# Attention scores from two fp32r parts, two heads at a time on row halves, in place of three bf16 parts with one head at a time

## The chip, the cores and the metric

The kernel runs on one core of one Trainium2 chip. The time is the device time of one launch in microseconds, the median of three runs. "The profiled execution" is one more launch, taken with the hardware profiler; all rows below are from it.

## What is computed

Eight batch elements of 512 rows by 256 columns go through three blocks with residuals: an mLSTM cross attention with four heads (stage A), a mixture of two multi-head attentions of 16 heads of 16 columns each, and a mixture of experts, two of eight chosen by a router (stage C). The change is in the middle block:

```python
n1 = _ln(x, ln1_g, ln1_b)
mha_probs = jax.nn.softmax(jnp.mean(n1, axis=1) @ mha_rw + mha_rb, axis=-1)
q = jnp.einsum('btd,mdhk->mbhtk', n1, mha_wq) + mha_bq[:, None, :, None, :]
kk = jnp.einsum('btd,mdhk->mbhtk', n1, mha_wk) + mha_bk[:, None, :, None, :]
v = jnp.einsum('btd,mdhk->mbhtk', n1, mha_wv) + mha_bv[:, None, :, None, :]
scores = jnp.einsum('mbhtk,mbhsk->mbhts', q, kk) / jnp.sqrt(jnp.float32(KD))
attn = jax.nn.softmax(scores, axis=-1)
ctx = jnp.einsum('mbhts,mbhsk->mbthk', attn, v)
```

Everything is fp32. There are 8 x 2 x 16 = 256 heads of 512 by 512 scores, each with a contraction of only 16.

## The kernel before

Each engine has its own program, written out by hand, and they meet through semaphores. The batch elements are pipelined. A *period* is one batch element's attention; in it run also stage A of the next element and stage C of the one before. A period has 128 slots, one for each score tile: 8 quads of four heads (`qq`), 4 row tiles (`g`), 4 heads (`j`). Three tables (`FIRST`, `MIDDLE`, `LAST`) say at which slot each other piece of work (`p0` to `p7` the K and Q projections, `v0`, `v1` the value projections, `cxT..`, `wo..`, `hid..`, `eo..` of stage C, `kT..`, `cd..`, `num..` of stage A) stands in each engine's program. The digit string `AHEAD` says how many maxima TensorE computes behind each slot. The MIDDLE table serves six of the eight periods.

A head's scores are computed twice. `maximum` (L880) makes a tile of 128 queries by 512 keys, of which VectorE takes the row maxima (L1411). When a quad's 16 tiles are done, `max_rows` transposes the maxima, VectorE splits them in two bf16 rows (L1419, L1421), and SyncE sends these as two more rows of Q (`send_rows`). `score` (L895) then makes the transposed tile of keys by queries with the maximum already subtracted, ScalarE takes the exponential into `prob` (L1710), and `values` (L910) multiplies it by V, four heads at once on column groups of 32, for two row tiles together in every eighth slot.

Fp32 accuracy comes from splitting. ScalarE writes the projection in bf16 (`high`, L1632), VectorE the residue (L1283), GpSimd the second and third bf16 part (`middle_low`, L1861 and L1863). SyncE stacks six products of parts along the contraction (`stack`), 16 rows each, so that one matmul of 96 rows (98 with the maxima) gives the score:

```python
TERMS_K = (0, 0, 1, 1, 0, 2)
TERMS_Q = (0, 1, 0, 1, 2, 0)
```

The first heads of the first element are stacked by matmuls with a choice matrix instead (`pick`, L665 and L680), 48 of them.

PSUM has seven banks for all this and one (`VB`) for the values. `Banks.take` gives each result the bank that is free earliest by the tables, and TensorE waits for its last reader. In the names of the trace all matmul results are `psum`; `kst`, `qst` are the stacks, `mx` the maxima.

## Time and profile before

| | |
|---|---|
| median of three runs | 1407.55 us (1404.99 to 1409.78) |
| profiled execution, whole time | 1407.98 us |
| its span, first to last instruction | 1406.2 us |
| TensorE busy | 1380.4 us, 98% |
| VectorE busy | 1074.6 us, 76% |
| ScalarE busy | 911.4 us, 65% |
| GpSimd busy | 361.0 us, 26% |
| granted TensorE clock, mean | 0.995 |

A busy time is the union of an engine's instructions. TensorE's instructions overlap in its pipeline and their ends are modelled, so the distance from one start to the next says more than the duration. A matmul with fp32 operands leaves two records in the trace, each with a weight load: 1024 matmuls at L910 are 2048 records. A bf16 matmul and a transpose leave one.

### The profile page before, as it was taken

How to read it: one execution, taken by the hardware profiler on the slowest of the kernel's cores; microseconds unless marked ns; L12 is line 12 of the kernel's file. 1: busy time of each engine (PE TensorE's matmuls, PEld its weight loads, DVE VectorE, ACT ScalarE, POOL GpSimd, SP SyncE). 2: the span in 40 equal slices, each digit the busy share in tenths (PEclk: the TensorE clock that was granted, in tenths of full speed). 3: DMA queues.
4: the chain of work that ended last, by engine and by line, in shares of the span. 5: the costliest groups of instructions: out<-in, count | busy, mean ns of one | idle time of the engine just before them, and what ended most of it. 6: DMA issues, size and time to landing. Idle time of an engine off the chain costs nothing. (4 is left out here: it accounts for less than half of the span.)

```text
span 1406.2 us, 22227 instructions
## 1 busy us (share of the span) xinstructions
PE 1380.4 (98%) x7666; PEld 714.5 (51%) x7666; DVE 1074.6 (76%) x2299; ACT 911.4 (65%) x1708; POOL 361.0 (26%) x351
## 2 busy tenths in 40 slices
PE   8999999999999999999999999999999999999989
PEld 6644445554455544456445654555445555354456
DVE  6789878977698777986879777897779868688631
ACT  3367567756667667776577666775676765657751
POOL 7422341302313223113322034132132222221000
PEclk9999999999999999999999999999999999999999
DMA  4065075321744136530662308441174415352002
GB/s 118 17 79 89 2 79 88 67 55 31 105 62 78 59 44 105 86 55 31 85 96 54 69 16 106 76 76 61 28 109 77 75 31 62 46 69 54 21 12 90
DMA packets 92307, 90.15 MB, mean 64 GB/s; under 512 B 16482, under 2 KB 87266, under 8 KB 91294
## 3 DMA queue, kind: packets, MB, share of 16 engines
q1 hardware_dynamic: 92196, 88.73, 38.1%
q8 instruction: 62, 1.02, 0.4%
q14 instruction: 49, 0.40, 0.1%
HBM read 35.05 MB, written 4.25 MB: 28 GB/s over the span
## 5 line engine op out<-in xcount | busy, mean ns | idle before, releaser
L1710 ACT ACTIVATE prob<-psum 128x512 f32<-128x512 f32 x1024 | 560.6, 600 | 317.9 <-PE psum L910 217.2
L1411 DVE TENSOR_REDUCE mx<-psum 128x1 f32<-128x512 f32 x1024 | 640.6, 681 | 77.8 <-PE psum L880 75.3
L895 PE MATMUL psum<-qst,kst 98*128 98x512 bf16 x1024 | 340.7, 382 | 2.3 <-DMA qst<-mrow 1.3
L880 PE MATMUL psum<-kst,qst 96*128 96x512 bf16 x1024 | 305.1, 381 | 5.5 <-DVE resid L1283 2.2
L910 PE MATMUL psum<-prob,vst 128*17 128x512 f32 x2048 | 246.6, 598 | 0.4 <-ACT prob L1710 0.2
L895 PEld LDWEIGHTS psum<-qst,kst 98*128 98x128 bf16 x1024 | 94.9, 98 | 202.8 <-issue 136.5
L880 PEld LDWEIGHTS psum<-kst,qst 96*128 96x128 bf16 x1024 | 97.5, 97 | 127.7 <-ACT prob L1710 17.1
L1861 POOL CAST parts<-resid 128x512 bf16<-128x512 f32 x64 | 39.4, 616 | 404.0 <-DVE resid L1283 404.0
L910 PEld LDWEIGHTS psum<-prob,vst 128*17 128x17 f32 x2048 | 46.7, 96 | 128.8 <-issue 109.8
L867 PE MATMUL psum<-w,cxT 128*128 128x256 f32 x448 | 105.1, 381 | 0.0
L848 PE MATMUL psum<-n2T,x 128*128 128x512 f32 x224 | 102.0, 592 | 0.0
L867 PEld LDWEIGHTS psum<-w,cxT 128*128 128x128 f32 x448 | 85.2, 191 | 15.8 <-DVE mx L1411 1.1
L1863 POOL TENSOR_TENSOR parts<-resid,parts 128x512 bf16<-128x512 f32 x64 | 74.5, 1164 | 5.1
L1757 POOL TENSOR_TENSOR rstd_a<-rstd_a,neghalf 128x4 f32<-128x4 f32 x24 | 24.5, 1031 | 178.8 <-DVE rstd_a L994 100.7
L1831 POOL TENSOR_TENSOR kin<-qbuf,onw 128x1024 f32<-128x1024 f32 (+1 forms) x8 | 16.5, 2059 | 203.4 <-DVE qbuf L1120 201.2
L1419 DVE TENSOR_SCALAR mrow<-psum 16x128 bf16<-16x128 f32 x64 | 17.5, 273 | 63.5 <-PE psum L481 63.5
L848 PEld LDWEIGHTS psum<-n2T,x 128*128 128x128 f32 x224 | 42.3, 190 | 44.9 <-issue 41.8
L730 PE MATMUL psum<-n1T,wk 128*128 128x512 f32 x128 | 60.9, 598 | 0.0
L504 PE MATMUL psum<-wv,n1T 128*128 128x256 f32 x256 | 60.7, 379 | 0.0
L730 PE MATMUL psum<-n1T,wq 128*128 128x512 f32 x128 | 60.2, 592 | 0.0
L504 PEld LDWEIGHTS psum<-wv,n1T 128*128 128x128 f32 x256 | 48.0, 189 | 10.3 <-ACT n2T L1687 1.6
L765 PE MATMUL psum<-wo,cxT 128*128 128x256 f32 x224 | 51.8, 379 | 0.0
(244 smaller groups left out, 1708.3 us busy)
## 6 DMA issues: line engine op xcount, KB each, us to landing
kst<-parts SPq DMA_DIRECT2D x186, 128.0 KB, 4.6
qst<-parts SPq DMA_DIRECT2D x186, 128.0 KB, 5.5
cmat<-G_dram SPq DMA_DIRECT2D x7, 1024.0 KB, 4.7
x<-in_L_ffn_fw SPq DMA_DIRECT2D x14, 512.0 KB, 3.6
w<-in_L_ffn_fw SPq DMA_DIRECT2D x14, 512.0 KB, 4.1
xbuf<-in_x SPq DMA_DIRECT2D x8, 512.0 KB, 5.2
kin<-in_ctx SPq DMA_DIRECT2D x8, 512.0 KB, 4.5
out<-acc SPq DMA_DIRECT2D x7, 512.0 KB, 3.9
```

The lines of the kernel that those rows point to most:

```text
L504: ins = e.matmul(psum[:, u.bank, i * H * KD:(i + 1) * H * KD], n1T[:, kc, t * P:(t + 1) * P], wv[:, kc, m, :], start=kc == 0, stop=kc == K ...
L730: ins = e.matmul(psum[:, u.bank, :], w_[:, kc, m, c * P:(c + 1) * P], n1T[:, kc, :], start=kc == 0, stop=kc == KC - 1)
L765: ins = e.matmul(psum[:, u.bank, 0:E], cxT[:, m, c, t * P:(t + 1) * P], wo[:, m, c, :], start=k == 0, stop=k == M * KC - 1)
L848: ins = e.matmul(psum[:, u.bank, :], w1_of(b, k)[:, kc, f * P:(f + 1) * P], n2T_of(b)[:, kc, :], start=kc == 0, stop=kc == KC - 1)
L867: ins = e.matmul(psum[:, u.bank, 0:E], hidden_of(b, k)[:, f, t * P:(t + 1) * P], w2_of(b, k)[:, f, :], start=f == 0, stop=f == FC - 1)
L880: e.matmul(psum[:, u.bank, :], qst[0:KROWS, h, t * P:(t + 1) * P], kst[0:KROWS, h, :], start=True, stop=True).then_inc(u.full, 1)
L895: e.matmul(psum[:, u.bank, :], kst[0:KROWS + 2, h, g * P:(g + 1) * P], qst[0:KROWS + 2, h, :], start=True, stop=True).then_inc(u.full, 1)
L910: ins = e.matmul(psum[32 * j:32 * j + VW, VB, :], vst[:, g, h, :], prob[:, g % 2, j, :], start=g == 0, stop=g == NT - 1, tile_position=(0, ...
L1411: e.tensor_reduce(mx[:, qq * QUAD + j, t:t + 1], psum[:, u.bank, :], AX, ALU.max).then_inc(u.free, 1)
L1710: e.activation(prob[:, g % 2, j, :], psum[:, u.bank, :], ACT.Exp).then_inc(u.free, 1)
L1861: e.tensor_copy(parts[:, n % 2, 1, :], resid[:, n % 2, :]).then_inc(split_mid, 1)
L1863: e.tensor_tensor(parts[:, n % 2, 2, :], resid[:, n % 2, :], parts[:, n % 2, 1, :], ALU.subtract).then_inc(split_lo, 1)
```

## The change

K and Q are split in two parts instead of three, in fp32r (four bytes): ScalarE writes the first, VectorE the residue straight into the second, and GpSimd's part is gone. Three products of parts (48 rows) replace six (96 rows). Even heads lie in partitions 0 to 63 and odd heads in 64 to 127 of the same free positions, and a matmul of an even head is followed at once by that of the odd head on the other half of the array's rows. For the maxima the two results go to two neighbouring banks (`take_two`), and one VectorE reduction reads both; a quad has 8 such pairs, and `AHEAD` counts pairs. One more VectorE copy a quad (`mxx`) duplicates the maxima before the transpose. Scores are made in pairs at even slots, each in its own bank and with its own exponential. All slot tables are new; `values` stands at slot 0 of eight instead of slot 1. The stack's DMAs are the same in number and bytes with lines twice as long.

```diff
-    TERMS_K = (0, 0, 1, 1, 0, 2)
-    TERMS_Q = (0, 1, 0, 1, 2, 0)
+    TERMS_K = (0, 0, 1)
+    TERMS_Q = (0, 1, 0)
...
-        kst = sb("kst", [P, M * H, S], BF16)
-        qst = sb("qst", [P, M * H, S], BF16)
+        kst = sb("kst", [P, M * H // 2, S])
+        qst = sb("qst", [P, M * H // 2, S])
+        kstR, qstR = kst[:].bitcast(F32R), qst[:].bitcast(F32R)
...
+    def take_two(self, name, until):
...
+        k = min(range(self.count - 1), key=lambda k: (max(self.until(k), self.until(k + 1)),
+                                                      max(self.order[k], self.order[k + 1])))
+        self.counts[k] += 1
+        one = self.uses[name] = self.hold(k, self.counts[k], until)
+        one.both = slice(k, k + 2)
+        return one, self.hold(k + 1, one.n, until, k)
...
             def maximum(b, qq, j, t):
...
-                u = take("max", b, qq, j, t)
-                e.matmul(psum[:, u.bank, :], qst[0:KROWS, h, t * P:(t + 1) * P], kst[0:KROWS, h, :], start=True,
-                         stop=True).then_inc(u.full, 1)
+                u = take_two("max", b, qq, j, t)
+                for par in range(2):
+                    own = slice(HALF * par, HALF * par + KROWS)
+                    ins = e.matmul(psum[:, u.both, :][:, par, :], qstR[own, h // 2, t * P:(t + 1) * P], kstR[own, h // 2, :],
+                                   start=True, stop=True)
+                ins.then_inc(u.full, 1)
...
             def score(b, qq, g, j):
...
-                u = take("score", b, qq, g, j)
-                e.matmul(psum[:, u.bank, :], kst[0:KROWS + 2, h, g * P:(g + 1) * P], qst[0:KROWS + 2, h, :], start=True,
-                         stop=True).then_inc(u.full, 1)
+                us = [take("score", b, qq, g, 2 * j + par) for par in range(2)]
+                for par, u in enumerate(us):
+                    own = slice(HALF * par, HALF * par + KROWS + 2)
+                    e.matmul(psum[:, u.bank, :], kstR[own, h // 2, g * P:(g + 1) * P], qstR[own, h // 2, :],
+                             start=True, stop=True).then_inc(u.full, 1)
...
-                e.scalar_tensor_tensor(out=resid[:, n % 2, :], in0=psum[:, u.bank, :],
+                e.scalar_tensor_tensor(out=partsR[:, n % 2, 1, :], in0=psum[:, u.bank, :],
...
-                e.tensor_reduce(mx[:, qq * QUAD + j, t:t + 1], psum[:, u.bank, :], AX, ALU.max).then_inc(u.free, 1)
+                e.tensor_reduce(mx[:, qq, :, j, t], psum[:, u.both, :], AX, ALU.max).then_inc(u.free, 1)
+                if j == PAIRS - 1 and t == NT - 1:
+                    e.wait_ge(u.free, u.n)
+                    src = mx[:, qq].rearrange("p r h t -> p r (h t)")
+                    e.tensor_copy(mxx[:], src.unsqueeze(2).to_broadcast([P, 2, 2, UNITS])).then_inc(maxima_in, 1)
...
-                e.activation(parts[:, n % 2, 0, :], psum[:, u.bank, :], ACT.Identity,
+                e.activation(partsR[:, n % 2, 0, :], psum[:, u.bank, :], ACT.Identity,
...
-            def middle_low(b, n):
...
-                e.tensor_copy(parts[:, n % 2, 1, :], resid[:, n % 2, :]).then_inc(split_mid, 1)
-                e.wait_ge(split_mid, q_ + 1)
-                e.tensor_tensor(parts[:, n % 2, 2, :], resid[:, n % 2, :], parts[:, n % 2, 1, :], ALU.subtract
-                                ).then_inc(split_lo, 1)
...
-            AHEAD="1300200300314230044012000010100221221000031300001011000104403001"
-                  "0020100321400001210130341010440001130110030202100012010003000000")
...
+            AHEAD="3000100100102220100220201010001000200110000102000002000000120221000"
```

In `pick` there are now 16 matmuls in place of 48.

**TensorE, a stretch of the second period around the experts' first products (`hid`, L848 before and L870 after).** L895 and L920 are scores, L880 and L904 maxima, L910 and L935 values, L481 and L514 transposes, L867 and L889 the experts' second products. Before:

```order
L910 MATMUL psum<-prob,vst 17x512 x8
L895 MATMUL psum<-qst,kst 128x512
L880 MATMUL psum<-kst,qst 128x512 x4
L848 MATMUL psum<-n2T,x 128x512 x2
L895 MATMUL psum<-qst,kst 128x512
L848 MATMUL psum<-n2T,x 128x512 x6
L481 MATMUL psum<-ident,mx 16x128
L895 MATMUL psum<-qst,kst 128x512
L867 MATMUL psum<-w,cxT 128x256 x4
```

Now:

```order
L935 MATMUL psum<-prob,vst 17x512 x8
L920 MATMUL psum<-qst,kst 128x512 x2
L904 MATMUL psum<-kst,qst 128x512 x4
L870 MATMUL psum<-n2T,x 128x512 x2
L904 MATMUL psum<-kst,qst 128x512 x4
L870 MATMUL psum<-n2T,x 128x512 x4
L514 MATMUL psum<-ident,mxx 32x128
L920 MATMUL psum<-qst,kst 128x512 x2
L904 MATMUL psum<-kst,qst 128x512 x2
```

Scores and maxima now stand in twos, one for each half of the rows, between work on the whole array. Each such border is a change of the array's tiling that was none before. Counted over TensorE's whole program, with scores and maxima, L565 and L602 (64 rows), the values and L715 (column groups of 32), L577 (of 64) and all else as four kinds: the kind changed 348 times before and changes 892 times now. Before, 173 changes led into whole-array work (162 of them into a score), 32 into 64 rows, 135 into 32 columns, 8 into 64 columns; now 314, 423, 135 and 20, and 102 of the 314 begin with a transpose. In one middle period it was 44 changes and is 114 now (54 into 64 rows, before 4; 40 into the whole array, before 22), in the first period 40 and 90.

**VectorE, the last maxima of a quad and the row split behind them.** L1411 and L1433 are the maxima. Before:

```order
L1411 TENSOR_REDUCE mx<-psum 128x1 x4
L1431 RECIPROCAL rden<-psum 128x16
L1434 SCALAR_TENSOR_TENSOR cx<-psum,mpc,rden 128x4x64
L1411 TENSOR_REDUCE mx<-psum 128x1 x7
L1419 TENSOR_SCALAR mrow<-psum 16x128
L1421 SCALAR_TENSOR_TENSOR mrow<-psum,mrow 16x128
```

Now:

```order
L1457 RECIPROCAL rden<-psum 128x16
L1460 SCALAR_TENSOR_TENSOR cx<-psum,mpc,rden 128x4x64
L1433 TENSOR_REDUCE mx<-psum 128x2 x4
L1437 COPY mxx<-mx 128x32
L1433 TENSOR_REDUCE mx<-psum 128x2 x2
L1445 CAST mrow<-psum 32x128
L1447 SCALAR_TENSOR_TENSOR mrow<-mrow,low,psum 32x128
```

A reduction now gives two columns, there are half as many, and the copy is new.

## Rows read from the trace of the kernel before

**Rows 1.** The page: span, busy times, busy tenths in 40 slices, granted clock.

```profile
span 1406.2 us, 22227 instructions
...
PE 1380.4 (98%) x7666; PEld 714.5 (51%) x7666; DVE 1074.6 (76%) x2299; ACT 911.4 (65%) x1708; POOL 361.0 (26%) x351
...
PE   8999999999999999999999999999999999999989
...
DVE  6789878977698777986879777897779868688631
...
PEclk9999999999999999999999999999999999999999
```

**Rows 2.** Windows, one a stage: length, then each engine's busy time.

```profile
0.00:81.00 81.00, 72.83 (x384) 48.94 (x385) 55.31 (x140) 29.40 (x63) 42.55 (x62) 0.98 0.22 61
81.00:218.00 137.00, 131.61 (x757) 58.60 (x755) 116.06 (x231) 92.20 (x182) 41.23 (x39) 0.99 0.52 66
...
551.00:716.00 165.00, 164.80 (x935) 84.71 (x933) 132.73 (x284) 113.47 (x212) 42.69 (x39) 1.00 0.42 68
...
1214.00:1347.00 133.00, 131.55 (x706) 61.75 (x707) 92.13 (x185) 88.21 (x159) 17.74 (x15) 0.99 0.26 41
1347.00:1406.00 59.00, 52.48 (x214) 35.60 (x212) 13.92 (x37) 18.29 (x30) 3.35 (x2) 0.97 0.17 54
```

**Rows 3.** Groups by line: busy us, mean ns, idle before and releaser.

```profile
L1411 DVE TENSOR_REDUCE mx<-psum 128x1 f32<-128x512 f32 x1024 | 640.6, 681 | 77.8 <-PE psum L880 75.3
L1710 ACT ACTIVATE prob<-psum 128x512 f32<-128x512 f32 x1024 | 560.6, 600 | 317.9 <-PE psum L910 217.2 <-PE psum L895 98.5
L895 PE MATMUL psum<-qst,kst 98*128 98x512 bf16 x1024 | 340.7, 382 | 2.3 <-DMA qst<-mrow 1.3 <-ACT prob L1710 0.3
L880 PE MATMUL psum<-kst,qst 96*128 96x512 bf16 x1024 | 305.1, 381 | 5.5 <-DVE resid L1283 2.2 <-DVE mx L1411 1.4 <-ACT prob L1710 1.2
L910 PE MATMUL psum<-prob,vst 128*17 128x512 f32 x2048 | 246.6, 598 | 0.4 <-ACT prob L1710 0.2
...
L1863 POOL TENSOR_TENSOR parts<-resid,parts 128x512 bf16<-128x512 f32 x64 | 74.5, 1164 | 5.1
...
L1861 POOL CAST parts<-resid 128x512 bf16<-128x512 f32 x64 | 39.4, 616 | 404.0 <-DVE resid L1283 404.0
...
L665 PE MATMUL psum<-parts,qst 128*96 128x512 bf16 x27 | 6.7, 379 | 0.1
...
L1038 DVE COPY cols<-psum 128x48 f32<-128x48 f32 x8 | 1.5, 193 | 2.1 <-PE psum L550 2.1
```

**Rows 4.** Timeline of TensorE, 501.3 to 504.9 us: start, length, work.

```profile
501.55 0.59 PE L880 MATMUL psum<-kst,qst 96*128 96x512 bf16 x2
501.98 0.38 PE L895 MATMUL psum<-qst,kst 98*128 98x512 bf16 x1
502.20 0.38 PE L880 MATMUL psum<-kst,qst 96*128 96x512 bf16 x1
502.51 1.91 PE L910 MATMUL psum<-prob,vst 128*17 128x512 f32 x16
504.35 0.61 PE L895 MATMUL psum<-qst,kst 98*128 98x512 bf16 x2
504.80 0.38 PE L880 MATMUL psum<-kst,qst 96*128 96x512 bf16 x1
```

**Rows 5.** Timeline of TensorE, 28 to 31 us, a run of row-half pairs.

```profile
28.46 2.06 PE L565 MATMUL psum<-qT,kT 64*128 64x128 f32 x32
```

**Rows 6.** Line L565 by itself, durations min/median/max.

```profile
L565 PEld LDWEIGHTS psum<-qT,kT x256: 182/188/188, 28.5 to 1109.5; 64*128 64x128 f32 x128
L565 PE MATMUL psum<-qT,kT x256: 272/272/373, 28.5 to 1109.6; 64*128 64x128 f32 x128
```

**Rows 7.** Waits: us in total, times, longest.

```profile
POOL parts L1861 <- DVE resid L1283: 404.0, 61, 23.3
ACT prob L1710 <- PE psum L910: 217.2, 115, 5.8
...
DVE mx L1411 <- PE psum L880: 75.3, 85, 2.5
...
PEld psum L880 <- ACT prob L1710: 17.1, 59, 1.7
...
PEld psum L880 <- DVE mx L1411: 6.4, 17, 1.7
```

More of the change, by code:

```diff
@@ L57, in until, with hold @@
         return self.latest[k].until if self.latest[k] is not None else -1000
+    def hold(self, k, n, until, at=None):
+        at = k if at is None else at
+        self.taken += 1
+        self.order[k] = self.taken
+        self.latest[k] = Use(k, n, self.full[at], self.free[at], self.latest[k], until)
+        return self.latest[k]
     def take(self, name, until):
@@ L63, in take @@
         self.counts[k] += 1
-        self.taken += 1
-        self.order[k] = self.taken
-        use = Use(k, self.counts[k], self.full[k], self.free[k], self.latest[k], until)
-        self.uses[name] = self.latest[k] = use
-        return use
+        self.uses[name] = self.hold(k, self.counts[k], until)
+        return self.uses[name]
+    def take_two(self, name, until):
+        assert name not in self.uses
+        k = min(range(self.count - 1), key=lambda k: (max(self.until(k), self.until(k + 1)),
[4 more added lines that the diff above has]
+        return one, self.hold(k + 1, one.n, until, k)
 class Steps:
@@ L378, in build @@
+            SP_S=slots(18, "s4:5 s5:11 s6 s7"),
+            AHEAD="1200102010002002210100120000200210010100000100012000010000021220"
+                  "1120010020010010102100021001001000000100300011000000000010200000")
         for plan in (FIRST, MIDDLE, LAST):
-            assert len(plan["AHEAD"]) == SLOTS and sum(map(int, plan["AHEAD"])) == SLOTS
+            assert len(plan["AHEAD"]) == SLOTS and sum(map(int, plan["AHEAD"])) == SLOTS // 2
             for engine in ("PE", "ACT", "DVE", "POOL", "SP"):
@@ L401, in freed_at @@
             if period is None or not 0 <= period < B:
-                return now + 1
+                return now + (2 if kind == "score" and which[-1] % 2 else 1)
             plan = FIRST if period == 0 else LAST if period == B - 1 else MIDDLE
@@ L478, in take, with take_two @@
                 return u
+            def take_two(*name):
+                both = banks.take_two(name, freed_at(clock[0], *name))
+                for u in both:
+                    if u.was is not None:
+                        e.wait_ge(u.was.free, u.was.n)
+                return both[0]
             def transpose(out_, in_, n):
@@ L1176, in stage_a @@
                     e.wait_ge(u.full, u.n)
-                    e.tensor_copy(qst[0:KROWS, 0, :], psum[0:KROWS, u.bank, :]).then_inc(u.free, 1)
+                    e.tensor_copy(qstR[:, 0, :], psum[:, u.bank, :]).then_inc(u.free, 1)
                 yield "mean"
@@ L1606, in move_pick @@
                 e.wait_ge(u.full, u.n)
-                e.activation((kst, qst)[which][0:KROWS, h, :], psum[0:KROWS, u.bank, :], ACT.Copy).then_inc(u.free, 1)
+                if which:
+                    e.activation(qstR[:, h, :], psum[:, u.bank, :], ACT.Copy).then_inc(u.free, 1)
+                else:
+                    e.wait_ge(shaped, 3)
+                    e.activation(kstR[:, h, :], psum[:, u.bank, :], ACT.Identity, bias=lift[:]).then_inc(u.free, 1)
             def decays(b):
@@ L1814, in stage_a @@
                 e.tensor_copy(mk[:, b % 2, 1, :], sa.rstd[:, 1, :]).then_inc(kept, 1)
-                for n in range(len(PIECES) // M if b else 3):
-                    yield f"s{n}"
-                    middle_low(b, n)
             def weigh(b):
@@ L2119, in sync_program @@
             a.upto(-9)
-            e.wait_ge(ones, 1)
-            for i in range(1, M * H // HC):
-                e.dma_start(kst[KROWS:KROWS + 2, i * HC:(i + 1) * HC, :], kst[KROWS:KROWS + 2, 0:HC, :]).then_inc(ones_in, 16)
+            e.wait_ge(ones, 2)
+            for par in range(2):
+                own = slice(HALF * par + KROWS, HALF * par + KROWS + 2)
+                e.dma_start(kst[own, HP + 1:M * H // 2, :],
+                            kst[own, HP:HP + 1, :].to_broadcast([2, M * H // 2 - HP - 1, S])).then_inc(ones_in, 16)
             until_maxima(a, first)
```

317 lines of the change are left out of this document (156 added, 161 removed), and 12 rows, old and new, of the table DVE_A.

## The prediction

> **What bounds the kernel now.** I read the page first: TensorE is busy in 98% of the span, VectorE in 76%, ScalarE in 65%, and the granted clock is 1.0 nearly throughout, which is the 2.4 GHz level [rows 1]. The windows show where that holds. In a middle period of 165 us TensorE is busy 164.8, VectorE 132.7 (80%), ScalarE 113.5 (69%). In the first period it is less plain, 131.6 and 116.1 of 137 us, VectorE at 85%. The last period is TensorE's again, and the head and the tail (140 us together) hold few scores [rows 2]. The waits say the same: ScalarE waits 217 us for values on TensorE and VectorE 75 us for maxima, while TensorE's waits for a free bank are 17.1 us (ScalarE) and 6.4 us (VectorE) [rows 7]. So TensorE's own stream sets the pace, and what a change takes from it comes off the time, until VectorE is next.
>
> Busy times say nothing of rates on a pipelined engine, so I take distances between starts. Two maxima from 501.55 and the score at 501.98 give 0.215 us for a bf16 matmul of 512 columns. The 16 records of values lie in four groups of four that run at once, 0.43 us a group (from 502.51 to 504.42, less 0.59 for the last one, are 1.32 us for three steps, the first a little longer) [rows 4]. A value matmul is two records [rows 3], so fp32 costs 0.86 us where bf16 costs 0.215, four times as much.
>
> **The change part by part.**
>
> *Scores and maxima.* 2048 matmuls of 0.215 us are 440 us [rows 3, 4]. They become 1024 pairs. That two matmuls on the two row halves run at once is in the trace: L565 issues 32 records, 16 pairs, in 2.06 us. Less the last one's 0.27 and 0.10 for a slow first (below), 15 steps take 1.69 us, 0.113 each [rows 5, 6], where 128 fp32 columns of one matmul alone take 0.107 (256 cycles at 2.4 GHz). A pair thus costs some 0.007 us more than one. What fp32r costs no row shows, and it is the largest unknown. The nearest rows on either side are bf16, 0.215 us for 512 columns, and one fp32 record, 0.43 us [rows 4]. I take 0.215: two records of 0.43 make a full fp32 product of four partial ones, so a partial product costs 0.215, and a split in parts rests on one partial product a matmul. A pair is then 0.222, 1024 are 227 us, and the saving is 213 us. At 0.43 the saving would be nothing (1024 x 0.437 = 447 us, 7 more).
>
> The Trainium skill states in "FP8 and Floating Point Precision", TensorE Precision Notes, that true FP32 takes four passes through the array, and that a reduced-precision mode reads the four bytes and truncates them. The trace agrees with the four passes (0.86 against 0.215 us); no run so far shows the reduced mode. By that page a pair would be at my 0.222.
>
> *Pick.* 48 matmuls of 0.215 become 16: 7 us less, all in the head [rows 3].
>
> *Borders between tilings.* This is what the change adds. From the maximum at 502.20 to the first value is 0.31 us instead of 0.215, and from there to the next score 1.84 instead of 4 x 0.43 = 1.72 [rows 4]. I read 0.095 us for a change in each direction and 0.012 for a first weight load of 17 columns that nothing hides. The count goes from 348 to 892: 544 x 0.095 = 52 us.
>
> *The first weight load behind a border.* With 128 four-byte columns it is longer. L565's matmuls last 272 ns and the first of a run 373 [rows 6]: 0.10 us, and both halves load at once, so a pair pays it once. 391 more entries into the 64-row kind at 0.10 are 40 us. The bound from below is the bf16 score behind a border, 0.012, which would make it 5 us; I take 0.10, since the stacks are now four bytes wide, as in that row. The 314 entries into whole-array work now meet fp32 loads where 162 of 173 met a bf16 score: 212 x 0.10 and 102 transposes at 0.03 (my choice between 0.012 and 0.10) are 24 us, less 2. Elsewhere a load of 188 ns [rows 6] lies beside a pair of 222 and costs nothing; were the pair shorter it would show.
>
> The Trainium skill's "TensorEngine Tiling (Array Packing)", Key Properties, says that changing the tiling mode drains the engine. The trace agrees and gives it the price of 0.095 us. Without that price the sum below would be 52 us lower.
>
> Sum for TensorE: -213 - 7 + 52 + 40 + 22 = -106 us. Of these a middle period has -26.6 (256 x 0.215 less 128 x 0.222), +6.7 (70 borders), +5 and +3, that is -12, from 166 us to 154; the first period -16, the last with the tail -11, the head -7.
>
> *VectorE.* A reduction of 512 elements takes 640.6 / 1024 = 0.626 us. The line's mean of 681 ns against 193 for a copy of 48 columns makes 1.05 ns an element, so 1024 elements take 0.626 + 0.538 = 1.164, and 512 of them 596 us: 45 less. The new copies are 64 x 0.19 = 12 us [rows 3]. VectorE comes to 1042 us, in a middle period to 128.6. The residue writes as much as before.
>
> *GpSimd, ScalarE, SyncE.* GpSimd loses 74.5 + 39.4 = 114 us [rows 3], but it sat waiting 404 us for exactly this work [rows 7]; nothing else becomes earlier than its slot. ScalarE keeps its 1024 exponentials. `stack` waits for two splits in place of three and sends as many bytes. All three at nothing. If a late stack were a cost now, the maxima would wait for it, and the 5.5 us that they wait in all name VectorE and ScalarE [rows 3].
>
> *New waits.* In the first period VectorE, at 112 us after the change, would stand at 93% of the 121 us left. If it keeps its present 85%, the period ends at 132, not 121: 11 us. In the middle VectorE rises from 80 to 83.5% of the period; between the shares that cost 0.2 us (80%) and 5.4 us (85%) of TensorE idle [rows 2] I take 1.5 us, 9 in six. A reduction now holds two banks for 1.2 us, and behind three pairs in one slot (`AHEAD`'s 3) the next score waits for VectorE; these are a few slots a period and I count them in that. Sum: +20.
>
> The profiled execution took 1408 us, 1.8 of it outside its span, and is within 0.5 of the median. 1408 - 106 + 20 = 1322, and I say 1320.
>
> **The rivals.**
>
> *Fp32r streams like an fp32 record (slower).* A pair takes 0.437 us at lines L904 and L920. Speaking for it: every four-byte record in these rows moves at two cycles a column [rows 4, 5], which a limit of reading four bytes would give as well as two partial products would. Against it: then a full fp32 product in two records would need four partial products in the time of two reads, possible only if a read serves two. TensorE's sum is then +7 - 3 + 52 + 40 + 22 = +118 and VectorE is idle more: 1525 us. The change turns from gain to loss when a pair costs 0.222 + 86 / 1024 = 0.306 us. Halves that do not overlap in this format would cost the same.
>
> *VectorE or the banks take over.* If VectorE can't get beyond its 80% of a middle period, a period is 128.6 / 0.8 = 161 us, 5 saved instead of 12; first 5, head 7, last and tail 11: 1408 - 53 = 1355, and to 1395 if pairs of banks are often late. For it: two neighbouring banks of seven are harder to get, and the first period shows TensorE idle at 85%. Against: VectorE's work falls as well. The Trainium skill's tiling page, PSUM Bottleneck, warns of just this: tiling speeds the array and not the emptying of PSUM. Only the first period of this trace bears it out so far.
>
> *Cheap weight loads.* If an fp32r load behind a border costs 0.012 us, 35 us more are saved: 1285, and 1267 without the new waits.
>
> *Nothing changes.* It would take a chain outside TensorE in every period. The page's busy digits are 9 in all but the ends [rows 1]; I give it no case of its own.
>
> **How the numbers follow.** My forecast (1290 to 1345) 0.64, VectorE or banks (1345 to 1395) 0.15, cheap loads (1267 to 1290) 0.08, fp32r at the fp32 rate (about 1525, or some way there) 0.13. The range 1270 to 1375 holds the first, most of the third and somewhat over half of the second, some 0.8. Faster by over 0.3% (about what a measurement of this kernel tells from no change): 0.84, with 0.03 of the last case, where banks cost almost all, going to the same, and 0.13 slower.
>
> **What would show it.** In the new trace: starts of a pair some 7 ns apart and pairs 0.222 us apart; 0.31 from a pair to work of another kind; the first matmul behind a border 0.10 longer; the reduction's busy time at 1.16 us each; middle periods of 154 to 157 us; GpSimd's busy time 114 us lower and no wait for it. Pairs 0.43 apart would make the prediction wrong outright; middle periods near 161 with TensorE waiting for maxima would make it wrong in size.

## The result and the profile after

The changed kernel takes 1509.17 us (median of 4 runs, 1499.85 to 1514.36) against 1408.66 us before (4 runs on the same chip): a ratio of 1.071, 95% interval 1.0651 to 1.0769. It is 7% slower, where the forecast was 1320 us and 6% faster. The profiled execution took 1514.36 us.

The page of the changed kernel, to be laid beside [rows 1]:

```profile
span 1512.3 us, 22468 instructions
...
PE 1400.0 (93%) x7634; PEld 716.7 (47%) x7634; DVE 1071.6 (71%) x1856; ACT 889.6 (59%) x1686; POOL 250.0 (17%) x231
...
PE   9888889999899998999989998999989999899889
...
PEclk9898899899899998999999998989989999899999
```

TensorE is no longer the engine that is always busy: 93% of the span, not 98%. The row of granted clock has gaps in it that were not there. And no other engine has come near its limit; VectorE is at 71%, lower than the 76% before. That is the picture of a kernel that waits in turns, not of one with a new bound.

The groups by line (busy us, mean ns, idle before and its releaser), beside [rows 3]:

```profile
L1744 ACT ACTIVATE prob<-psum 128x512 f32<-128x512 f32 x1024 | 554.0, 602 | 367.2 <-PE psum L935 273.0
L1433 DVE TENSOR_REDUCE mx<-psum 128x2 f32<-128x1024 f32 x512 | 608.1, 1219 | 182.9 <-PE psum L904 180.4
L920 PE MATMUL psum<-qst,kst 50*128 50x512 f32 x1024 | 244.9, 492 | 43.5 <-DMA qst<-mrow 25.5
L935 PE MATMUL psum<-prob,vst 128*17 128x512 f32 x2048 | 282.9, 674 | 0.9 <-ACT prob L1744 0.9
L904 PE MATMUL psum<-kst,qst 48*128 48x512 f32 x1024 | 223.0, 455 | 47.4 <-DVE mx L1433 22.9
```

The reduction is as forecast: 608.1 / 512 = 1.19 us each, where 1.164 was said. What is new stands at the right. TensorE sat idle 43.5 us before scores (2.3 before the change) and 47.4 before maxima (5.5). The values have not changed, yet their mean rose from 598 to 674 ns. That is the clock: those that start at the full clock have a mean of 597 ns in the new trace too.

Windows, one a stage (head, first, the second of the six middle ones, last, tail), beside [rows 2]:

```profile
0.00:79.00 79.00, 68.50 (x352) 47.51 (x353) 53.10 (x138) 25.32 (x55) 36.91 (x65) 0.94 0.23 64
79.00:233.00 154.00, 135.80 (x759) 60.43 (x757) 114.78 (x175) 92.02 (x182) 23.59 (x19) 0.89 0.40 58
...
417.00:597.00 180.00, 168.62 (x944) 85.68 (x943) 133.50 (x230) 112.08 (x213) 29.18 (x23) 0.95 0.36 64
...
1316.00:1454.00 138.00, 127.91 (x718) 61.26 (x718) 90.49 (x138) 86.86 (x162) 10.57 (x7) 0.99 0.23 40
1454.00:1512.00 58.00, 51.96 (x214) 35.23 (x210) 13.90 (x37) 18.12 (x30) 3.32 (x2) 0.97 0.16 55
```

The head is 2 us shorter and the tail 1. The first stage went from 137 to 154 us (132 was forecast; its clock is 0.89), the six middle ones from 165-167 to 176-184, the last from 133 to 138. VectorE's work in a middle stage is what it was (133.5 us beside 132.7), in a stage 15 us longer; the forecast had it fall to 128.6.

TensorE's timeline from 276 to 284 us shows the change at work, and its price:

```profile
276.83 0.51 PE L920 MATMUL psum<-qst,kst 50*128 50x512 f32 x2
...
277.17 0.40 PE L904 MATMUL psum<-kst,qst 48*128 48x512 f32 x2
...
277.41 0.40 PE L920 MATMUL psum<-qst,kst 50*128 50x512 f32 x2
...
278.60 0.50 PE L920 MATMUL psum<-qst,kst 50*128 50x512 f32 x2
...
278.98 0.72 PE L904 MATMUL psum<-kst,qst 48*128 48x512 f32 x4
...
281.61 0.80 PE L920 MATMUL psum<-qst,kst 50*128 50x512 f32 x2 [1.91 <-DMA qst<-mrow]
...
282.34 1.91 PE L935 MATMUL psum<-prob,vst 128*17 128x512 f32 x8
```

Two matmuls of 512 columns, 0.40 us together, start 0.24 us apart from the next two (277.17 to 277.41). So fp32r does run at the bf16 rate, and two halves at once. The first pair behind a border takes 0.34 (276.83 to 277.17), 0.10 more, as forecast. Then the score at 281.61 waits 1.91 us for its maxima rows; and the values behind it move at half speed. Eight of the sixteen records take 1.91 us, where all sixteen took 1.91 in [rows 4].

What the engines waited for (us in total, times, longest), beside [rows 7]:

```profile
DVE mx L1433 <- PE psum L904: 180.4, 163, 5.8
...
PE psum L920 <- DMA qst<-mrow: 25.5, 13, 2.8
...
PE psum L904 <- DVE mx L1433: 22.9, 43, 1.4
...
PEld psum L904 <- ACT prob L1744: 20.6, 33, 1.8
```

VectorE waits for TensorE's maxima for 180 us in all (75 before), and TensorE waits for VectorE's banks: both sit idle, at different moments.

The mean clock of the profiled execution is 0.944. With two levels, 1.2 and 2.4 GHz, the share at the lower one is 2 x (1 - 0.944) = 11%, or 169 us of 1512; before, at 0.994 to 0.996, it was 11 to 17 us. Most of the 29 falls come in or just behind a wait of TensorE, like the one at 281.61 us. Those at 38.5, 332.1 and 1052.3 us come behind rows of short matmuls (L625, L635) that had kept it busy. The four runs of this one kernel show how time and clock go together: 1499.85 us at 0.958, 1507.21 at 0.949, 1511.13 at 0.947, 1514.36 at 0.944, that is about 1.0 us for each 0.001. If that holds up to 1, some 50 us of the 100 lost go with the clock (an estimate from four runs, in which waits and clock may have changed together).

A last view of my own: the distances between successive starts on TensorE, where nothing holds them up, summed for the whole kernel, and what is above them. Before: 1363 us of clean steps, 6 for the lower clock, 40 of longer steps. After: 1279, 68 and 186 (the three overshoot the span by 3 and 21 us). By this view the stream did become 84 us shorter, and some 190 to 210 us came on top. It is an estimate: which step counts as clean is my choice for each kind of neighbours, and another choice gives another split.

### The profile page after: what moved, and what is told of

Same layout as the page of the kernel before. It is cut to its first block, busy times and chain, and to the rows that moved or that the text cites. A ratio compares the mean times of both kernels' runs of the same rounds, so it can differ in the third digit from the quotient of the medians.

```text
span 1512.3 us, 22468 instructions
## 1 busy us (share of the span) xinstructions
PE 1400.0 (93%) x7634; PEld 716.7 (47%) x7634; DVE 1071.6 (71%) x1856; ACT 889.6 (59%) x1686; POOL 250.0 (17%) x231
## 4 chain that ended last, share of the span: by engine, by line
PE 67%; DMA 10%; DVE 9%; issue 9%; SPq 3%; ACT 3%; POOL 0%; DVEq 0%; ACTq 0%; POOLq 0%
PE psum L935 14%; PE psum L920 9%; PE psum L904 7%; PE psum L889 7%; PE psum L870 7%; DVE mx L1433 6%; DMA qst<-mrow 5%; PE psum L752 5%; PE psum L514 5%; PE psum L537 4%; PE psum L787 3%; DMA kst<-parts 2%; SPq L2007 2%; PE psum L625 2%; DMA G_dram<-mid 2%
## 5 line engine op out<-in xcount | busy, mean ns | idle before, releaser
L1744 ACT ACTIVATE prob<-psum 128x512 f32<-128x512 f32 x1024 | 554.0, 602 | 367.2 <-PE psum L935 273.0
L1433 DVE TENSOR_REDUCE mx<-psum 128x2 f32<-128x1024 f32 x512 | 608.1, 1219 | 182.9 <-PE psum L904 180.4
L920 PE MATMUL psum<-qst,kst 50*128 50x512 f32 x1024 | 244.9, 492 | 43.5 <-DMA qst<-mrow 25.5
L935 PE MATMUL psum<-prob,vst 128*17 128x512 f32 x2048 | 282.9, 674 | 0.9 <-ACT prob L1744 0.9
L904 PE MATMUL psum<-kst,qst 48*128 48x512 f32 x1024 | 223.0, 455 | 47.4 <-DVE mx L1433 22.9
L920 PEld LDWEIGHTS psum<-qst,kst 50*128 50x128 f32 x1024 | 100.1, 192 | 226.2 <-issue 166.7
L904 PEld LDWEIGHTS psum<-kst,qst 48*128 48x128 f32 x1024 | 104.4, 193 | 153.9 <-issue 93.1
L935 PEld LDWEIGHTS psum<-prob,vst 128*17 128x17 f32 x2048 | 49.5, 103 | 139.7 <-issue 121.1
L889 PE MATMUL psum<-w,cxT 128*128 128x256 f32 x448 | 109.8, 391 | 0.0
L870 PE MATMUL psum<-n2T,x 128*128 128x512 f32 x224 | 103.8, 605 | 0.0
L889 PEld LDWEIGHTS psum<-w,cxT 128*128 128x128 f32 x448 | 81.7, 191 | 22.3 <-issue 11.2
L870 PEld LDWEIGHTS psum<-n2T,x 128*128 128x128 f32 x224 | 40.2, 189 | 48.4 <-issue 48.3
L1949 POOL TENSOR_TENSOR acc<-x,xbuf 128x1024 f32<-128x1024 f32 x7 | 20.5, 2932 | 250.8 <-DVE x L1323 250.8
L1737 ACT ACTIVATE cxT<-psum 128x512 f32<-128x512 f32 x56 | 33.4, 598 | 41.4 <-PE psum L870 40.7
L1666 ACT ACTIVATE parts<-psum,bks 128x512 fp32r<-128x512 f32 x32 | 22.1, 691 | 58.4 <-PE psum L752 36.8
```

The source lines that it names most:

```text
L870: ins = e.matmul(psum[:, u.bank, :], w1_of(b, k)[:, kc, f * P:(f + 1) * P], n2T_of(b)[:, kc, :], start=kc == 0, stop=kc == KC - 1)
L889: ins = e.matmul(psum[:, u.bank, 0:E], hidden_of(b, k)[:, f, t * P:(t + 1) * P], w2_of(b, k)[:, f, :], start=f == 0, stop=f == FC - 1)
L904: ins = e.matmul(psum[:, u.both, :][:, par, :], qstR[own, h // 2, t * P:(t + 1) * P], kstR[own, h // 2, :], start=True, stop=True)
L920: e.matmul(psum[:, u.bank, :], kstR[own, h // 2, g * P:(g + 1) * P], qstR[own, h // 2, :], start=True, stop=True).then_inc(u.full, 1)
L935: ins = e.matmul(psum[32 * j:32 * j + VW, VB, :], vst[:, g, h, :], prob[:, g % 2, j, :], start=g == 0, stop=g == NT - 1, tile_position=(0, ...
L1433: e.tensor_reduce(mx[:, qq, :, j, t], psum[:, u.both, :], AX, ALU.max).then_inc(u.free, 1)
```

## The experiments

Unless another is named, edits are to the changed kernel (1509.17 us). A time without an interval is one run.

**Twice the work.** Each pair is issued twice into its banks: the maxima (first run), the scores (second run). Nothing is left out.

```
-                for par in range(2):
+                for par in (0, 1, 0, 1):
```

> The changed kernel with each pair of maxima matmuls issued twice into the same two banks: 512 x 0.21 = 108 us more work for TensorE and nothing else. Theory A (TensorE's own stream is about 1280 us, as the start distances add up; the rest of the 1512 is waits for banks and rows, and a clock that falls to half after them): part of the added work fills waits and the granted clock rises above 0.944, so the time rises by 20 to 70 us only. Theory B (the pairs and the borders cost more than their start distances show, and TensorE's stream is still the bound): the whole 108 us is added, 1610 to 1625 us, at the same clock.

> The changed kernel with each pair of score matmuls issued twice into the same banks, 512 x 0.21 = 108 us more for TensorE, and each score ready 0.21 us later. Theory A: 20 to 80 us more, and a higher granted clock. Theory B: 108 us more or somewhat over, the same clock.

Measured 1536.80 us at a clock of 0.982, and 1554.96 at 0.975, both in theory A's range. Each adds 512 pairs, 110 us or more (0.215 to 0.24 us a pair), and costs 28 and 46 us. A bound TensorE would have paid all of it. So some 65 to 90 us of TensorE's time are idle or slow enough to be filled, and filling them raises the clock.

**Lighter readers, one at a time.** The first run leaves half of the keys out of the maxima: the reduction reads 256 of the 512 columns of each of its two banks. (Its text speaks of the edit less exactly; this is what ran.) The second lets scores contract 48 rows, without the two maxima rows, and wait for none until the last two quads; the exponential is of a hundredth of the score. The third does both.

```
-                e.tensor_reduce(mx[...], psum[:, u.both, :], AX, ALU.max)
+                e.tensor_reduce(mx[...], psum[:, u.both, 0:S // 2], AX, ALU.max)
...
-                if g == 0 and j == 0:
+                if g == 0 and j == 0 and q_ >= B * NQ - 2:
                     e.wait_ge(rows_in[q_ % 2], 32 * (q_ // 2 + 1))
```

> The changed kernel with the maxima reduced over the first 256 columns of one bank in place of 1024 of two (three quarters and more of the keys are left out of the maximum): VectorE has some 0.8 us less at each of 512 reductions, about 400 us in all. Theory A with VectorE as the late one (pairs of banks are held until it comes): waits of TensorE for maxima and rows nearly go, the clock comes back to 0.99, and the time falls to 1350 to 1400. Theory B: no change beyond 1%.

> The changed kernel with scores that contract over the 48 rows alone, so that they need neither the maxima's rows nor their DMA (the maximum is not subtracted, and the exponential is that of a hundredth, to stay finite); the rows are still computed and sent. If the rows' arrival is the main wait (it shows as 28 us directly, and as a clock at half behind it), the time falls by 50 us or more, to 1460 or less. If banks held by VectorE and ScalarE are the main wait, it falls by 10 to 35 us, to 1475 to 1500. Theory B: no change.

> The runs without rows and with the short reduction together (scores contract 48 rows and wait for no maxima rows, exponential of a hundredth, reduction over 256 columns of each bank); the exponential stays 512 columns wide. Apart they gave -36 and -41 us against 1509. If the two are waits of their own, 1432 us; if they share the clock that the waits cost, less than that, 1400 to 1425 us; the rest down to the 1386 us of the run with light exponentials too is ScalarE's share.

Measured 1468.22, 1473.64 and 1429.88 us: -41, -36 and -79 beside 1509. The two add up, as the third expectation had it (1432). Neither alone is the loss. The expectation for the first (1350 to 1400) missed: VectorE's reductions are one wait of several. With the short reduction TensorE's waits for VectorE ahead of maxima fall from 22.9 to 3.8 us, but those for the rows rise from 25.5 to 32.2 and those for exponentials, ahead of maxima, from 16.8 to 25.0. The second run lies between its two ranges (1460 or less, 1475 to 1500).

**All readers light.** As the third, and the exponential takes 256 of 512 columns; the rest of the probabilities is 1.

> This kernel lightens everything that reads TensorE's results and keeps TensorE's own stream: the scores contract 48 rows without the two rows of the maxima (so they wait for no such rows, but at the very end), the reduction of the maxima reads 256 of the 512 columns of each of its two banks, and the exponential writes the first 256 of 512 columns, of a hundredth of the score; the rest of the probabilities is 1. Every matmul and weight load stays. Theory A (the 100 us over before are waits behind VectorE, ScalarE and the transfer of the maxima rows, and the half clock that follows sparse stretches; TensorE's own stream is about 1280 to 1300 us): 1290 to 1340 us, with a granted clock of .98 or more and middle stages of 150 to 158 us. Theory B (the new matmuls on row halves, their borders and exposed loads are themselves dearer than forecast, and TensorE is as busy as before): 1430 us or more with middle stages of 170 us or more.

Measured 1385.96 us at 0.993. One middle stage by the windows:

```profile
539.00:703.00 164.00, 159.16 (x933) 82.16 (x932) 102.06 (x227) 84.14 (x210) 29.13 (x23) 1.00 0.40 69
```

Between the two theories: the clock is back at 1.00 and 123 us are gone, but a stage is 164 us, not 156. Half-size readers leave something standing, and the next question was what.

**The place of the DMAs.** SyncE issues its DMAs in the order of its program. Ahead of the maxima rows of quad 2 it sends the load of G (1 MB, a table of stage A's gates copied to all partitions), ahead of those of quad 7 the six DMAs of the last Q stack. In the kernel before the load of G stood ahead of the rows too (issued at 422.8 and 424.6 us), the Q stack behind them (536.5 after 533.7), and TensorE waited 1.3 us for rows in all. One run sends both behind the rows; in a second one the readers of G come later too.

```
-            SP_A=slots(-1, "ctx:4 x:3 gi:14 G:64 s0:6 s1:2 s2:2 s3"),
+            SP_A=slots(-1, "ctx:4 x:3 gi:18 G:60 s0:6 s1:2 s2:11 s3"),
```

The second run besides, in `ACT_A` and `DVE_A` of the middle plan:

```
- ... fa:16 mask00:0 mask01 mask02:0 mask03:6 mask10 ...
+ ... fa:22 mask00:0 mask01 mask02:0 mask03:0 mask10 ...
...
- ... M:7 cols gend:8 dec:7 ...
+ ... M:7 cols:8 gend:1 dec:7 ...
```

> Only two places in the order of SyncE's DMAs change: the last stack of Q (six DMAs) goes behind the sending of the maxima rows of quad 7 instead of ahead of it, and the store and load of G behind the sending of those of quad 2. Theory C (the rows' DMAs queued behind large ones are a main part of the loss: scores then wait 2.0 and 2.2 us in each of the eight batches, and the clock falls to half after them): 4.2 us by 6 to 8 batches is 25 to 34 us, with some of the clock's 60 to 85 us given back: 1450 to 1480 us. Theory D (the scores are held by banks and exponentials just behind, so the wait moves to the next reader): 1495 to 1515 us.

> The order of the run with the rows first, and the two readers of G (VectorE's copy of its last columns, ScalarE's masks) seven and six slots later, since in that run the wait had moved to them (VectorE 30 us, ScalarE 26 us). Theory C (the place in SyncE's queue costs 25 to 34 us of waits and some of the clock, once nothing else waits for the load of G): 1460 to 1485 us, with middle stages of 172 to 177 us. Theory D (the wait moves once more, to banks or exponentials just behind): 1495 to 1515 us.

The first measured 1507.65 us, ratio to before 1.0724 (1.0689 to 1.0758): no gain, as theory D said. TensorE no longer waits for rows, but VectorE and ScalarE wait for G. In that run:

```profile
DVE gend L1071 <- DMA cmat<-G_dram: 30.1, 6, 5.5
```

```profile
ACT cmat L1589 <- DMA cmat<-G_dram: 25.8, 6, 4.8
```

The changed kernel has 11.4 and 7.1 us there. The exponentials stand behind the mask in ScalarE's program and are late with it, and the values wait 20 us for them (0.9 before the edit). The wait was moved, not removed. With the readers later both waits are gone: 1484.34 us, ratio 1.0524 (1.0479 to 1.0568), 25 us less, clock 0.964, just within theory C's range. The place in the queue is thus a real part of the loss, about a quarter.

**Fewer bursts.** The slots with three pairs of maxima are broken up as far as the order of banks allows, with the last Q stack behind the rows; then also G behind them.

```
-            AHEAD="3000100100102220100201010001000200110000102000002000000120221000"
-                  "1000000202000100100200330100020011010000000101020020010010000000")
+            AHEAD="3000100100111220100201010001000200110000102000002000000210122000"
+                  "1000000202000100100210230100011011010000000101020020010010000000")
```

> The table of how many pairs of maxima stand in each slot is changed so that no slot has three pairs but one where the order of banks leaves no choice (the same number of pairs in all), and the last stack of Q goes behind the rows of quad 7. Theory A (TensorE waits at the slots of three pairs, 1.3 us at slot 84, .9 at slot 0, and for the rows of quad 7, 2.2 us): 3 to 4.4 us of each middle stage, 20 to 35 us in all, 1475 to 1490 us. Rival D (what is spread is waited for elsewhere, since VectorE's reductions are the same 596 us and its banks come free in order): 1495 to 1515 us.

> The two kernels before together: maxima pairs spread over the slots, the last stack of Q behind the rows of quad 7, the store and load of G behind those of quad 2. Theory A and C (waits add up and are independent): 1435 to 1470 us, still above the kernel before. Rival D (the wait moves to the next reader): 1490 to 1515 us. If the clock is what the loss hangs on, the granted clock rises from .95 to over .97 and the time falls by more than the sum of the waits taken away.

The first measured 1517.69, 1530.15, 1541.54 and 1552.80 us (median 1535.84), wide apart; the shortest is only 3 us above the longest of the changed kernel. The second measured 1562.90 us (1.1102, 1.106 to 1.1144; clock 0.929). Worse, and worse together, and outside every range that was expected. In the profiled execution of the first (1517.69 us), TensorE's waits for VectorE's banks at the maxima rose from 22.9 to 35.1 us, which fits a pair that, moved by one slot, met a bank not yet read. Why the other executions are longer, and the second kernel longer still, is not shown.

**Work put into the waits.** Eight useless pairs ahead of the first score of quads 2 and 7, in its own banks; then the wait for the rows.

```
+                if g == 0 and j == 0 and qq in (2, 7):
+                    for par, u in list(enumerate(us)) * 8:
+                        own = slice(HALF * par, HALF * par + KROWS)
+                        e.matmul(psum[:, u.bank, :], kstR[own, h // 2, 0:P], qstR[own, h // 2, :], start=True, stop=True)
+                    e.wait_ge(rows_in[q_ % 2], 32 * (q_ // 2 + 1))
```

> Useless work is put where TensorE waits for the maxima rows: ahead of the first score of quads 2 and 7 the same two banks are filled eight times by pairs of 48-row matmuls (16 x .215/2 = 1.7 us each time, 16 times, 27 us of work in all), which wait for the banks alone; only then the wait for the rows. Nothing else changes. Theory E (the short waits let the granted clock fall to half, and that costs 60 to 85 us by itself): the filler lies inside the 2.0 and 2.2 us waits, the granted clock rises from .944 to .96 or more, and the time falls to 1470 to 1495 us although work was added. Rival F (the clock follows the sparse matmuls on row halves, not the waits): clock .94 to .95, 1505 to 1540 us.

TensorE's timeline there:

```profile
285.65 2.11 PE L921 MATMUL psum<-qst,kst 48*128 48x512 f32 x16 [0.35 <-ACT prob L1749]
288.00 0.49 PE L925 MATMUL psum<-qst,kst 50*128 50x512 f32 x2 [0.25 <-DMA qst<-mrow]
288.42 1.91 PE L940 MATMUL psum<-prob,vst 128*17 128x512 f32 x16
```

The sixteen records take 2.11 us, the wait for rows has shrunk to 0.25 and the sixteen value records run at full speed. Measured 1502.16 us, ratio 1.0654 (1.0609 to 1.0698), clock 0.963: 16 x 2.11 = 34 us of work were added and the time is 7 us lower in the medians (the intervals of the two ratios overlap). The clock rose as theory E says, but its gain of 15 to 40 us did not come; the time lies between the ranges of E and F. The waits that the filler could lie in were too short for it: TensorE's waits for the rows were 25.5 us in the changed kernel and are 2.2 here, so some 23 of the 34 us replaced waiting and 11 were added. At about 1 us for each 0.001 the clock gives back 19 us, and the sum is near the 7 us measured (an estimate).

**Row halves undone.** All matmuls of maxima and scores (but the first 16 maxima) contract rows 0 to 112. The two of a pair run one after the other. Each result is the sum of two heads' products.

```
-                    own = slice(HALF * par, HALF * par + KROWS + 2)
+                    own = slice(0, HALF + KROWS)
```

> The pairing on row halves is undone and all else of the change kept: every matmul of maxima and scores (but the 16 of the first quad ahead of the loop) contracts rows 0 to 112, that is both heads' stacks and what lies between, so two of a pair run one after the other and no border to a row half is crossed. Left out: each result is the sum of two heads' products, the maxima rows are sent to rows that no matmul reads (the scores still wait for them), the exponential is of a hundredth; VectorE and GpSimd clear some rows at the head, which may cost up to 20 us there. Banks, reductions, exponentials, the places of all work and the DMAs are those of the changed kernel. By its own steps: about 1,000 pairs of the changed kernel take .215 us more each (+215 us), and the borders and first loads fall from about 157 us to some 41 (as before), so TensorE's own stream is 1279 + 215 - 116 = about 1380 us. Theory H (the loss is TensorE idling in bursts behind readers that are no faster, and the half clock that row-half bursts and waits bring; a longer but even and dense stream hides most of both): 1420 to 1470 us with a clock of .98 or more, so less than the changed kernel although TensorE has 100 us more to do. Rival I (the readers, two banks at once, and the new places are the bound whatever the matmuls cost): 1500 us or more; the waits of 186 us stay, and 1550 us if they add.

Measured 1548.18 us, ratio 1.0994 (1.0948 to 1.1041), clock 0.986. One middle stage:

```profile
605.00:790.00 185.00, 178.17 (x936) 106.25 (x934) 133.57 (x228) 111.09 (x211) 29.15 (x23) 0.99 0.35 61
```

The number is rival I's (1550), and theory H's 1420 to 1470 missed. But the 100 us that I had put on the stream were too few: such a matmul starts 0.231 us after the one before, not 0.215, and some 400 times, behind other work, 0.31 to 0.34. That is 2,000 x 0.016 + 400 x 0.1 = 72 us more (an estimate from these distances). TensorE then has some 175 us more to do, and the kernel takes 39 more, some 5 of them in the head, where the extra clearing stands (the first maxima start at 67.9 us, not 62.4). As in the doubled runs most of what is added goes into the waits and the clock, as H says; the total alone doesn't tell the two apart.

**Wait instructions.** A matmul carries one wait; a pair waits for two banks ahead of its first matmul, so one wait is an instruction of its own. Counted over the traces there are 608 before and 1556 after. The next three runs give each matmul its own wait: in the changed kernel, in the one with G's readers later, and in the one with light readers. The fourth writes each wait for a bank twice in the kernel before, for scores and maxima.

```
-                us = [take("score", b, qq, g, 2 * j + par) for par in range(2)]
-                for par, u in enumerate(us):
+                for par in range(2):
+                    u = take("score", b, qq, g, 2 * j + par)
```

> The changed kernel, result and all; only where TensorE waits for a bank is moved. A matmul carries one wait; the second is an instruction of its own in TensorE's queue, 51 ns in the trace, and a weight load issued behind it starts about 76 ns later. The trace of before has 608 of these, that of after 1556, because a pair waits for both of its banks ahead of its first matmul. Here each of the two matmuls waits for its own bank, which takes away some 950 to 1020 of them. In the run with light readers, steps between pairs without such an instruction are .231 us, with one .31 at the least. Theory J (the single waits lay the four-byte weight loads of 183 ns bare; .04 to .08 us each): 40 to 80 us less, 1430 to 1475 us, and more if the clock rises with it. Rival K (the long steps are real waits for the bank, whoever carries the wait): 1495 to 1515 us.

> The same edit on the kernel with rows first and G's readers later (1484 us). Theory J: 1400 to 1445 us, near the kernel before. Rival K: 1475 to 1490 us. If this and the places are independent, it gains as much as the same edit alone.

> The same edit on the kernel with light readers (1386 us; it leaves out the same parts: no maxima rows in the scores, half of each reduction, half of each exponential). Theory J: 1305 to 1345 us, since there most of what is left above TensorE's own stream of about 1280 us would be those instructions. Rival K: 1375 to 1390 us.

> The kernel before with every wait for a bank ahead of a score or a maximum written twice, the second already met: some 2,040 instructions of 51 ns more in TensorE's queue, with two-byte weight loads. If such an instruction costs its time whatever stands behind it, 2,040 x .05 to .08 = 100 to 160 us: 1510 to 1570 us. If it only lays bare loads that fill their slot (183 of 231 ns for four bytes, less for two), as steps of .215 to .218 us with one in between in the trace of before suggest: 1405 to 1430 us.

Line L503, the wait of `take`, by itself, has 516 such instructions in the changed kernel. In the first of these runs:

```profile
L503 PEldq EVENT_SEMAPHORE  x67: 51/51/1936, 48.9 to 1420.3; - x67
```

All in all 595 are left. The time is 1496.46 us, ratio 1.0603 (1.0555 to 1.0652); then 1484.70 us beside 1484.34, and 1388.69 beside 1385.96. The kernel before with 2,593 of them takes 1407.15 us. Theory J falls, and all four times lie in the ranges of its rivals. At most 13 us are the price of these instructions, in one of three kernels, and there the intervals of the two ratios touch. So the longer steps between pairs have another cause.

**Next to no readers, in both kernels.** The reduction reads 32 of 512 columns of each bank, the exponential 64 of 512, of a hundredth; the scores contract no maxima rows. The same on the kernel before.

```
-                e.activation(prob[:, g % 2, j, :], psum[:, u.bank, :], ACT.Exp)
+                e.activation(prob[:, g % 2, j, 0:S // 8], psum[:, u.bank, 0:S // 8], ACT.Exp, scale=0.01)
```

> The changed kernel with readers that take next to nothing: the reduction of the maxima reads 32 of the 512 columns of each of its two banks, the exponential 64 of 512 columns (of a hundredth of the score; the other probabilities stay 1), and no score contracts or waits for maxima rows but at the very end. All matmuls and weight loads stay. Theory A (TensorE's own stream, summed from distances between starts that nothing holds up, is about 1280 us; what the run with half-size readers, 1386 us, had above it were still waits for banks in runs of several pairs): 1290 to 1325 us, granted clock .99. Rival L (the stream itself takes some 1380 us: long steps between pairs, borders or weight loads that the distances miss): 1365 to 1390 us.

> The same edits on the kernel before (reduction over 32 of 512 columns, exponential over 64, of a hundredth, no maxima rows in the scores but their wait at the very end). By the distances between starts its own stream is 1363 us, its waits 40 us, most of them in head, tail and first stage: 1365 to 1385 us. With the run beside it, this gives the difference of the two streams without readers: theory A 60 to 85 us in favour of the changed kernel (the forecast was 106), rival L none.

Measured 1359.58 and 1391.39 us. A reduction now takes 222 ns:

```profile
L1433 DVE TENSOR_REDUCE mx<-psum 128x2 f32<-128x64 f32 x512 | 111.6, 222 | 298.4 <-PE psum L904 294.2
```

One middle stage of each, the changed kernel first:

```profile
529.00:690.00 161.00, 158.22 (x942) 83.27 (x942) 73.04 (x230) 64.94 (x212) 29.12 (x23) 1.00 0.40 71
```

```profile
544.00:709.00 165.00, 164.85 (x940) 85.91 (x939) 77.14 (x286) 70.87 (x214) 42.84 (x39) 1.00 0.42 69
```

Both theories missed. Where the readers cost nothing the changed kernel is 32 us faster: neither the 60 to 85 of theory A nor the none of rival L. By the same estimate from distances its stream is 1284 us of clean steps with 86 of longer ones and 11 of clock (that sum overshoots by 23), the kernel before 1361 with 27 and 4. The clock is 0.991 here with every pair still on row halves, so row halves by themselves don't bring it down.

## Why the prediction was wrong

By the last two runs the loss has two parts. 1509.2 - 1408.7 = 100.5 us is -32 for the streams (1359.6 - 1391.4) and +132 for what reads them: (1509.2 - 1359.6) - (1408.7 - 1391.4) = 149.6 - 17.3.

- **The step that failed: "New waits", with its sum of +20.** The runs show +132 in its place, which includes the clock. The prediction took VectorE's share of a middle stage (80 to 83.5%) as the measure and so got 1.5 us a stage. But VectorE was busy 133.5 of 180 us, far from full, and TensorE still waited. The forecast did see bursts ("behind three pairs in one slot") but counted them inside that 1.5 us. What counts is the moment. A pair takes two banks in 0.24 us and a reduction gives both back after 1.2 us; TensorE is faster in exactly those bursts and no faster between them. The runs divide the 150 us above 1359.6: half of the reductions 41, the maxima rows 36 (two values that add up), half of the exponentials 44, the rest of the reading 26. Of these, 25 us could be had back by two places in SyncE's queue and two behind them.
- **A term that was left out: the granted clock.** It was read as 1.0 and kept. After the change it is 0.944, and the four runs put about 50 us on it (an estimate, and a part of the +132, not beside it). As far as the runs show it follows the waits and sparse stretches: it came back to 0.96 to 0.99 in the runs that made readers or rows' waits lighter, and as high where matmuls were only added (0.963 to 0.986), with bank waits of VectorE hardly shorter (22.7 us with whole height). So 2 us of waiting can cost more than 2 us.
- **The sum for TensorE, -106, was too large.** Distances give -77 to -84 of clean steps (an estimate), and the two kernels without readers' cost -32. The rate was right (0.231 to 0.24 a pair, 0.222 said), the first load behind a border was right (0.34 against 0.23 us), and borders and loads were counted well: by distances they came to 52 us and 64 (52 and 62 said). What the sum lacks are steps between pairs that are longer even with readers of 222 ns (86 against 27 us). Part of those are waits for banks and for a late exponential; which part is the stream's own stays open.
- **Smaller terms.** The reduction came nearly as said (1.19 us, 1.164 said), and so did GpSimd's busy time (-111 us); whether its loss had an effect on the time was not tested. VectorE's sum did not: 1071.6 us where 1042 was said. The reductions are 12 us above the forecast, and the new copies take 23.1 us, 0.36 each, where 12 was said. The head came out 2 us shorter, not 7, and last stage and tail together 4 us longer, not 11 shorter.
- **The rivals.** "Fp32r streams like an fp32 record" gave 1525 us and lies nearest to the result, for the wrong reason: its sign, pairs 0.43 us apart, isn't there. "VectorE or the banks take over" named the mechanism, also the Trainium skill's ("TensorEngine Tiling (Array Packing)", PSUM Bottleneck): tiling speeds the array and not the emptying of PSUM. The trace agrees, with 43.5 and 47.4 us idle ahead of scores and maxima. Its price was far too low, though: it still had 5 us saved a middle stage, in place of 12, and 11 to 18 were lost. It was worked out from busy shares again, and knew no DMA and no clock.

No version here beats the kernel before; the best with its full result is 1484.3 us. A bank and a reduction for each single maximum, and pairs spread quite evenly over the slots, weren't tried, so it stays open how much a wholly new table of places would give.

## What to carry to other kernels

When a change speeds up the producer, don't ask whether the consumer has the hours; ask for the longest run of results in a row, how many banks it fills, and when the first comes back. Count two neighbours that come free together as later than either (an argument: no run here gives each maximum its own bank and reduction). If such runs also let the array fall idle for a microsecond or two at a time, price the clock with it, and look at the order of any in-order DMA queue that feeds the waiting instruction.

To find how long a stream takes without its readers, shrink them to almost nothing, in both kernels. Here that one pair of runs gave 32 us where the sum of distances had promised 60 to 85.

## What the runs showed of the hardware

- Fp32r matmuls of 512 columns on 48 or 50 rows: two halves at once, steps of 0.231 us within a run of pairs; on 112 rows, alone, 0.231 us too, where bf16 has 0.215. The profile shows them as one f32 record each, an fp32 product as two. The first behind other tiling takes 0.335 us.
- Some 2,000 separate wait instructions more in TensorE's queue, 51 ns each, cost nothing that can be seen (1407.15 us).
- The clock: stretches at the lower level in and behind waits of only 2 us (281.61 us above), 169 us in all, in a kernel whose TensorE is 93% busy. With 34 us of useless work in those waits the clock was 0.963 and the time no longer.
